# Sixteen sequences, then sixteen experts: three experts' weights loaded over finished buffers, and identity products on TensorE in the last round

## The reference, cut to what matters

```python
x = layernorm(x + L0_attn(x))   # selective-scan mixer, 64 heads, state 64
x = layernorm(x + L0_ffn(x))    # int-quantised SwiGLU feed-forward, hidden 704
x = layernorm(x + L1_attn(x))   # cumulative attention, then SwiGLU with hidden 1024:
#   uv = y @ w_swiglu.T; u, g = split(uv); x + u * silu(g) @ w_out.T
x = layernorm(x + L1_ffn(x))    # mixture of 16 experts, top 4, hidden 448:
#   logits = x @ gate_inp.T; w = softmax(top4(logits))
#   y = sum_e w[n, e] * (silu(x @ W_gate[e].T) * (x @ W_up[e].T)) @ W_down[e].T
```

## Time and profile before

| | us |
|---|---|
| median of three executions | 1888.61 |
| profiled execution | 1896.84 |
| its span, first to last instruction | 1895.0 |
| TensorE busy (products) | 1704.0, 90% |
| VectorE busy | 1315.2, 69% |
| wait of TensorE in front of the tile count (line 882) | 4.69 |
| end of the last product of the layers block | 1279.85 |
| first product of the experts block | 1300.72 |
| share of the span in the chain that ended last: TensorE up and gate (line 1701) | 13% |
| the same: TensorE down (line 1716) | 7% |

### The profile page before, as it was taken

The page is one execution under the profiler, slowest core; times in us unless marked ns, Lnnn a source line. Parts: engine busy times, 40 slices in busy tenths (PEclk is TensorE's granted clock), DMA queues, the critical chain, the costliest instruction groups (busy, mean ns, idle before and its releaser), DMA issues. The chain is left out here.

```text
span 1895.0 us, 34676 instructions
## 1 busy us (share of the span) xinstructions
PE 1704.0 (90%) x8516; PEld 1210.1 (64%) x8517; DVE 1315.2 (69%) x3087; ACT 741.1 (39%) x1400; POOL 863.7 (46%) x823
## 2 busy tenths in 40 slices
PE   4699999999999999999999998864999999999980
PEld 2368778768777677777787676651655656665650
DVE  4788888888988988888888887331444444444445
ACT  3335445345455354444553453211222323233323
POOL 2033353353343433433533433123666777777764
PEclk7899999999999999999999999886999999999995
DMA  6524133132242241341331322637999999999998
GB/s 202 183 91 128 44 108 103 50 114 85 65 128 66 84 128 52 98 122 35 115 97 57 118 70 75 271 140 202 166 166 164 172 175 176 167 173 173 172 147 271
DMA packets 369688, 244.14 MB, mean 129 GB/s; under 512 B 250656, under 2 KB 348256, under 8 KB 369248
## 3 DMA queue, kind: packets, MB, share of 16 engines
q1 hardware_dynamic: 303840, 171.56, 36.0%
q0 software_dynamic: 40704, 67.40, 19.1%
q10 hardware_dynamic: 25088, 4.50, 1.8%
HBM read 122.67 MB, written 68.78 MB: 101 GB/s over the span
## 5 line engine op out<-in xcount | busy, mean ns | idle before, releaser
L1701 PE MATMUL pu<-w_all,xh 128*128 x1728 | 361.1, 357 | 35.3 <-DMA xh<-xin 31.2
L1701 PEld LDWEIGHTS pu<-w_all,xh 128*128 128x128 bf16 x1728 | 169.5, 99 | 184.1 <-issue 63.1
L1834 POOL DMA_INDIRECT sums_dram<-yo,meta_in x144 | 232.1, 1612 | 113.3 <-issue 48.0
L840 PE MATMUL pb<-x1T,w_sw 128*128 128x256 f32 x1024 | 233.4, 384 | 0.7 <-ACT x1T L959 0.7
L840 PEld LDWEIGHTS pb<-x1T,w_sw 128*128 128x128 f32 x1024 | 195.7, 192 | 50.3 <-issue 15.0
L1785 DVE TENSOR_TENSOR hid<-pu,gate 128x448 f32<-128x448 f32 x144 | 90.0, 625 | 176.3 <-PE pu L1701 71.7
L1716 PE MATMUL py<-w_all,hh 128*128 x1584 | 201.5, 274 | 6.7 <-DMA hh<-hs 4.1
L1716 PEld LDWEIGHTS py<-w_all,hh 128*128 128x128 bf16 x1584 | 152.2, 98 | 59.7 <-issue 19.5
L1821 POOL DMA_INDIRECT xin<-x_dram,meta_in x144 | 144.1, 1001 | 73.0 <-issue 40.5
L655 PE MATMUL pa<-w_in,xT 128*128 128x512 f32 (+1 forms) x384 | 165.6, 573 | 9.3 <-DMA bc_bias<-in_bc_bias 8.4
L778 PE MATMUL pb<-x1T,w_gu 128*128 128x256 f32 x704 | 164.8, 386 | 6.9 <-DVE hT L1393 6.2
(11 more groups left out here) (249 smaller groups left out, 2917.4 us busy)
## 6 DMA issues: line engine op xcount, KB each, us to landing
w_all<-split_ug SPq DMA_DIRECT2D x17, 896.0 KB, 9.8
w_stage<-in_w_ug SPq DMA_DIRECT2D x64, 224.0 KB
split_ug<-w_parts SPq DMA_DIRECT2D x64, 224.0 KB
w_all<-split_dn SPq DMA_DIRECT2D x17, 512.0 KB, 10.4
xg_dram<-xg SPq DMA_DIRECT2D x16, 512.0 KB, 2.8
w_stage<-in_w_dn SPq DMA_DIRECT2D x32, 256.0 KB
split_dn<-w_parts SPq DMA_DIRECT2D x32, 256.0 KB
rows<-sums_dram SPq DMA_DIRECT2D x32, 256.0 KB, 5.5
```

The source lines that it names most:

```text
L840: last = mm(pb[:, 1 + j % 2, w * T:(w + 1) * T], w_sw[:, c, o:o + P], x1T[:, c, :], start=c == 0, stop=c == DC - 1)
L1701: last = mm(pu[:, 2 * b + w, 0:EH], xh[:, m % XS, DC * xp + c, :], w_ug[:, bass.ds(e, 1), wp, c, w * EH:(w + 1) * EH], start=n == 0, stop= ...
L1834: nc.gpsimd.indirect_dma_start(out=sums_dram[m % 2], out_offset=bass.IndirectOffsetOnAxis(ap=meta[:, m, 0:1], axis=0), in_=yo[:, m % XS, : ...
```

## The change

Two things change.

Weights: a third boundary `EARLY_C = 15` is added. The buffers under experts 12 to 14 are those of the SwiGLU stage, and their loads are issued by SyncE in the layers block, in a new piece CG after C9 of sequence 15 (C9 stores the tokens for the gathers), when x3 of sequence 15 is ready. The condition in the experts block now selects expert 15 alone, at step 0, after `turn_x(3)` and `turn_h(0)`; the second load of expert 11 is gone.

TensorE: `keep_warm(s, n)` issues n products of the identity with itself (fp32, 128 x 128 x 128) into a PSUM bank that nobody reads then, only for sequence 15. They stand in front of the waits of C7 (14), B1T (7), B3T (14), the first half of B4 (6), B5T (9) and C8 (11), then 16 in front of the tile count, 40 behind it at the end of the block, and 22 at the start of the experts block.

```diff
-EARLY_A, EARLY_B = 8, 12
+EARLY_A, EARLY_B, EARLY_C = 8, 12, 15
...
-    "SP": ("CE C7 A0 N0 A2 WL.0 WL.1 AR C9 WL.2 WL.3 WL.4 WL.5 CF"),
+    "SP": ("CE C7 A0 N0 A2 WL.0 WL.1 AR C9 CG WL.2 WL.3 WL.4 WL.5 CF"),
...
+            def load_third(s):
+
+                if isinstance(s, int) and s == nseq - 1:
+                    sp.wait_ge(x3_ready.sem, x3_ready.at(s))
+                    for e in range(EARLY_B, EARLY_C):
+                        load_weights(sp, e, w_all, weights_in, split_ug, split_dn)
...
+            def keep_warm(s, n):
+
+                if isinstance(s, int) and s == nseq - 1:
+                    for _ in range(n):
+                        mm(pa[:, 3, 0:P], ident, ident, start=True, stop=True)
...
             def b1_first(s):
+                keep_warm(s, 7)
                 transposes(x1, x1_ready, rows_transposed, s)
...
             def b3_first(s):
+                keep_warm(s, 14)
                 transposes(x2n, x2n_ready, rows_transposed, s)
...
                 if part == 0:
+                    keep_warm(s, 6)
                     pe.wait_ge(kq_exp.sem, kq_exp.at(s, 2 * NT - 1))
...
             def b5_first(s):
+                keep_warm(s, 9)
                 transposes(yc, yc_ready, rows_transposed, s)
...
             def c7(s):
+                keep_warm(s, 14)
                 transposes(x3, x3_ready, x3_transposed, s, 3)
...
             def c8(s):
+                keep_warm(s, 11)
                 pe.wait_ge(choice_ready.sem, choice_ready.at(s))
...
+            keep_warm(nseq - 1, 16)
             pe.wait_ge(passed_ready.sem, passed_ready.at(0))
...
+            keep_warm(nseq - 1, 40)
...
-                if isinstance(r, int) and UN * r + m + 2 < NE - EARLY_B:
-                    load_weights(sp, EARLY_B + UN * r + m + 2, w_all, weights_in, split_ug, split_dn)
+                if isinstance(r, int) and 0 <= UN * r + m < NE - EARLY_C:
+                    load_weights(sp, EARLY_C + UN * r + m, w_all, weights_in, split_ug, split_dn)
...
+            for _ in range(22):
+                mm(pu[:, 3, 0:P], ident[:, :], ident[:, :], start=True, stop=True)
             steps(pe, step, 0, ntile + 3)
```

More of the change, by code:

```diff
@@ L370, in layers_block @@
         yc = sb("yc", [P, NT, D])
+        assert nc.sbuf_base >= w_start + EARLY_C * WB
         w_route = sb("w_route", [P, DC, NE])
@@ L640, in load_second @@
                         load_weights(sp, e, w_all, weights_in, split_ug, split_dn)
-            run_skewed(sp, ORDER["SP"], nseq, {"CE": load_first, "CF": load_second, "A2": store_xg, "N0": lambda s: None if isinstance(s, int) and s == 0 else load_x(s), "AR": load_rest, "A0": load_rows, "C7": store_x3, "C9": store_parts, "WL": store_piece})
+            def load_third(s):
[3 more added lines that the diff above has]
+                        load_weights(sp, e, w_all, weights_in, split_ug, split_dn)
+            run_skewed(sp, ORDER["SP"], nseq, {"CG": load_third, "CE": load_first, "CF": load_second, "A2": store_xg, "N0": lambda s: None if isinstance(s, int) and s == 0 else load_x(s), "AR": load_rest, "A0": load_rows, "C7": store_x3, "C9": store_parts, "WL": store_piece})
             for n in range(2):
```

## The result

| | before | after |
|---|---|---|
| median of 20 runs each, same chip | 1888.11 us (1880.38 to 1895.69) | 1874.46 us (1863.16 to 1887.94) |
| ratio | | 0.9927, 95% interval 0.991 to 0.9944 |
| profiled execution: time, span | 1896.84, 1895.0 us | 1868.15, 1866.3 us |
| granted clock, mean | 0.956 | 0.973 |

The change makes the kernel 13.7 us (0.7%) faster; 18.7 was forecast from the trace and 1870 us as the time. The two profiled executions lie 28.7 us apart, twice the difference of the medians, so I compare them by stage. Columns: start of the products of `B1T` in sequence 15; from there to the block barrier (the semaphore events of line 291 with which the other engines pass it, 0.1 to 0.2 us behind the end of GpSimd's drain); barrier to the first product of tile 0; tile 0 to tile 6; tile 12 to the end. All in us, from TensorE's timeline and the rows of line 291.

The account below looks back on a forecast made before the run. TensorE's chain of waits and products, with clock falls, bounds the last round; late `xh` behind loads bounds the experts' head. 12.0 (head) + 6.7 (clock) = 18.7 us off the median 1888.6 gives 1870 us, range 1862 to 1882.

Parts of the forecast that it names:

- B1 at full clock: Last layer round: B1's 44 records at 0.221 us take 9.7 instead of 11.16 us, a gain of 1.4 us.
- B3T and B3: Last round at full clock: B3T gains 0.5 us (0.66 instead of 1.12), B3 2.2 us (3.5 instead of 5.75).
- B5T and B5: Last round at full clock: B5T gains 0.5 us, B5 1.6 us (14.1 instead of 15.79).
- logits, less C8's overrun: End of last round: logits gain 0.8 us at full clock, less 0.3 us because C8's 11 products overrun their wait.
- last round: Layers block, sequence 15: identity products filling TensorE's waits hold the clock at full and gain 6.7 us together, at most 7.5.
- head, tile 0 to 6: Start of experts block: with loads moved away, tile 6 starts at 1322.5 instead of 1334.49, 12.0 us less (bounds 7.7 to 16).
- The price of a product: An identity product on TensorE is two fp32 records: 0.24 us at full clock, 0.46 us at the low one.
- The rival that ends slower: Identity products run at 1.2 GHz, overrun the waits and hold no clock: 20.9 us lost against 12.0 won, 1897.5 us; chance 0.06.
- the clock is lost in part: Rival: after B4 TensorE still idles, B5 and one other place start low, 3 us missing, 1873 us; chance 0.17.
- The barrier: End of layers block: barrier stays at 1290.5 us, 40 products end at 1289.4; rival that loads delay it: 1880 us, chance 0.09.
- The 22 behind the barrier: Start of experts block: 5.2 us of products, hidden before tile 0; cost nothing, no gain counted since tile 0 stays cold.
- What is late next: Head of experts block: turn_x(4), behind turn_h(0) and expert 15's load on SyncE, lands around tile 3's end, costing at most 1 us.

Follow-up runs that it names:

- the changed kernel's second trace: The changed kernel itself, unedited, run again on another chip beside two variants: median 1862.34 us, ratio 0.991 to the kernel before (1879.62).
- The late load: Changed kernel with expert 15's load issued at step 6, behind turn_h of tile 6, instead of step 0: 1867.22 us against 1884.06 before, ratio 0.9915.

## Why the prediction was right or wrong

| step | forecast | measured (before, after) |
|---|---|---|
| B1 at full clock | 1.4 | 1.4 (11.16, 9.76) |
| B3T and B3 | 2.7 | 2.5 (x2n to yc 17.7, 15.2) |
| B5T and B5 | 2.1 | 0.4 (yc to x 28.4, 28.0) |
| logits, less C8's overrun | 0.5 | 0.75 (x to C8 5.54, 4.79) |
| C8 to barrier | 0 | 0.1 (17.0, 16.8) |
| last round | 6.7 | 5.2 (90.8, 85.6) |
| head, tile 0 to 6 | 12.0 | 6.0 (33.8, 27.8) |
| sum of the last two | 18.7 | 11.2 by stage, 13.7 by medians |

**The price of a product** was right: 28 records took 3.29 us, 0.235 us a product, against 0.24 forecast. The rival that ends slower, which decided from 0.38 us on, is out.

**The clock.** It was held at three of the four places where it had fallen, and lost at one. That is the rival "the clock is lost in part" at the very place that it named (behind B4, before B5), at 1.7 us instead of 3. Fourteen products hold it there, and it falls further on instead.

**The barrier** did not move behind the last scatter. The loads were through by 1264 and the stretch from the last transposes to the barrier was 21.6 us, 22.5 before. The 40 products behind the tile count ended at 1270.1, 0.6 us before GpSimd's drain did.

**The 22 behind the barrier** cost nothing and gave nothing, as argued: the clock fell at the end of TensorE's wait of 4.68 us, and the first four tiles took 10.91 us with them, 10.83 without. Thirty-six held it in the kernel that had them.

**The head** is the step that failed: 12.0 were forecast and 6.0 measured (8.8 in the changed kernel's second trace). The prediction put it in "What is late next": turn_x(4), queued behind turn_h(0) and the load of expert 15, "at most 1 us". It cost 5.90 us of waiting and the clock for tile 4 (2.2 us more). Without these 8.1 the head would have beaten the forecast, 19.7 us from tile 0 to 6 against 22 (19.5 were measured with the load elsewhere). That is a second error, the other way: the forecast took 11.4 us for tiles 0 to 2 at the pace of before, and they took 8.5, as the clock was low only up to about 1284.2 (0.94 over 1284 to 1286). I had counted that load as DMA time that lies beside the work, 3.3 us, and not asked how long a transpose right behind it in one queue takes to land: 9.05 us. The row for that was at hand, the 11.17 us of the earlier trace rows, with five loads beside it; I took it as the effect of all five, where one is enough for most of it (6.55 to 9.50 in five traces with the load at step 0). The late load shows that the load is the cause (0.38 us in front of tile 4), and the other kernels with a late load show that the cost then stands elsewhere. The mark set for this, no wait for `xh` over 3 us behind tile 0, was missed, and so was that of 22 us from tile 0 to tile 6.

So the time came out within the range because the direction and the price were right and the two errors, 1.5 and 6 us, were small against a range of 20 us. By stage the gain was 60% of the forecast; by the medians it was 13.7 us, 10.6 to 17.0 by the interval, which leaves the forecast of 18.7 out. By the same stages the products in the last round were about half of the gain and not a third.

## What to carry to other kernels

A load that leaves a crowded place takes its cost along unless the new place is idle: three went where DMA had nothing to do and cost nothing that the stages show, the one that stayed cost 8.1 us of waiting and low clock. Ask of each large DMA which small one is queued right behind it and what waits for that. Moving or splitting the load moved the wait here, and none of the places tried in the block was free. Products that overrun a wait in front of an operation on the path cost their full time (2.1 us for 9 too many), and a fall of the clock that is prevented in one place may come a little later, so read the stage sum and not the one row.

## What the runs showed of the hardware

- One load of 1.41 MB made a transpose right behind it on its queue land after 9.05 us instead of 3.20 (6.55 to 9.50 in five traces with the load at step 0, 9.98 to 12.17 in three with it at step 6; 8.16 behind a load of 512 KB). A record load of 2 KB on another queue landed after 4.97 and 5.04 us instead of 1.79.
- TensorE's clock went from 1.00 to 0.50 at about 381.5 us of the kernel before while TensorE was 100% busy, in a layer round that took 76.2 instead of 72.9 us. Executions of one kernel, 15 to 25 us apart, differ in part by how many such rounds they have: 0, 2 or 4 in the traces here, and the start of `B1T` in sequence 15 lies at 1185 to 1188, 1192 to 1195 and 1199 to 1200 us with them.
- The same last round without identity products took 90.8 and 93.2 us in two executions, as the clock was low for different lengths of time: B1 took 11.16 and 12.77 us, and 9.76 at the full clock.
- Identity products in ordinary form hold the clock as the kernel's own products do (1.00 from 1186 to 1222 us, with four waits filled by them).
